# A fused attention and FFN kernel: the loop over head pairs in groups of six slots, contexts on column halves, output projection ahead in whole banks

## The chip, the cores and the metric

The kernel runs on one core of a Trainium2 chip. The metric is the device time of one execution in microseconds, a median of several runs. The five engines (TensorE, VectorE, ScalarE, GpSimd, SyncE) each take their instructions in program order and wait for one another by semaphores.

## What is computed

Two layers over x (4 x 256 tokens of 256 features, 1024 tokens in all). The change touches the first sublayer, an attention with 16 heads whose keys and values come from a context of 64 features:

```
def _L0_xattn_ref(hidden_q, kv_c, Wq, w_kc_q, w_kc_kv, W_qr, W_kr, Wo):
    q_hk = (hidden_q @ Wq.T).reshape(Bv, Sv, H, K)
    q_big = jnp.einsum('bshk,hkq->bshq', q_hk, w_kc_q)
    q_big = _apply_rope(q_big, ...)
    kv_r = _apply_rope(kv_c, ...)
    q_r = jnp.einsum('bshq,hqr->bhsr', q_big, W_qr)
    k_r = jnp.einsum('bld,hdr->bhlr', kv_r, W_kr)
    attn = jax.nn.softmax(jnp.einsum('bhsr,bhlr->bhsl', q_r, k_r), axis=-1)
    ctx_c = jnp.einsum('bhsl,bld->bhsd', attn, kv_r)
    ctx_lat = jnp.einsum('bhsd,hkd->bhsk', ctx_c, w_kc_kv)
    return ctx_lat.transpose(0, 2, 1, 3).reshape(Bv, Sv, H * K) @ Wo.T
x = x + _L0_xattn_ref(_layernorm(x), ctx_512, ...)
x = x + _L0_ffn_ref(_layernorm(x), ...)      # matmuls in emulated fp8, scales by absolute maxima
x = x + _L1_xattn_ref(ctx_512, ctx_512, mask_SxS2_bk1, mask_BxS2_bf0, _layernorm(x), ...)
x = x + _L1_ffn_ref(_layernorm(x), ...)
```

## The kernel before

Heads are taken in 8 pairs. The products of weights are folded once for each pair: `prep(f, 0)` and `prep(f, 1)` make `w1` (the two halves of Wq times w_kc_q), `prep(f, 2)` makes `wqk`, `prep(f, 3)` makes `wkvo`. All four use one PSUM bank, `pW`, in turn; ScalarE copies each out (`fold_copy`), VectorE takes the rounding rest (`w1_low`, `wqk_low`), and the next `prep` waits for that. `latent_q(m)` makes a third (r = 0, 1, 2) of the latent queries of 512 tokens in the single bank `pq`; `rope(m)` on VectorE rotates it, `join` on GpSimd adds the parts, `rope_high_xy` and `rope_high_z` on ScalarE round them, `rope_lows` on VectorE makes the rest. `latent_u(n, r)` multiplies by `wqk` into the bank `pu`; `u_copy` (ScalarE) and `u_low` (VectorE) bring it to SBUF. A unit is one head of one batch (256 x 256 scores): `scores` on TensorE, the row maximum on VectorE (L806), two exponentials on ScalarE (L549), a reciprocal on VectorE (L811), `norm_probs` on GpSimd (L392), `turn_probs` on TensorE (transposes, L1179), the copy `probT` on ScalarE (L540), and `context` on TensorE (L1191), which for the first head of a batch writes zeros into the lower half by way of zero columns kept in `kva`. VectorE copies the context of a batch to `cT` (L823). At the end `project` (L1196) multiplies `cT` by `wkvo` and sums over the 8 pairs.

The order of each engine is written out by hand: a loop `for it in range(1, PAIRS + 1)` over 12 slots of half a `latent_q` step each; in slots 1 to 8 a unit's scores are taken, three slots later it is transposed, four slots later its context comes. `latent_q` has the even slots, `latent_u` the odd slots with m % 3 below 2, `prep` slots 1, 3, 5 and 7. In the last iteration, 21 of the 64 projections (`EARLY = 3` token tiles) are spread over the slots, two calls each. After the loop TensorE projects the remaining tiles one by one, VectorE adds each to x and takes its statistics:

```
                elif i in (1, 2) and f:
                    pe.wait_ge(w1_parts, 2 * f + i)
...
            sp.wait_ge(scores_ready, NUNIT * PAIRS)
            sp.dma_start(ctx1[:], ctx_t[0:HK1, 0:TOK]).then_inc(ctx1_here, 16)
            ...
            sp.dma_start(mA[:], attn_mask.rearrange("(a p) s -> p a s", p=P)).then_inc(d_mask, 16)
```

SyncE's second piece waits for all 64 units' scores, since the tiles it fills share memory with the loop's. GpSimd, after its last `norm_probs`, waits for `d_mask`, makes the mask bias of the second attention (L430 to L436), a bias tile (L442, L443), scales `wg` (L449) and only then has the `pow` for the inverse deviation of the 1024 rows (`power(2)`, L365), for which VectorE waits in `newton(2)`.

During iterations 1 to 6 VectorE and ScalarE also find the absolute maxima of the two FFN weights and cast them to fp8 steps, in pieces (L855, L857, L568, L569).

Of the kernel before, what the change touches and what calls it, by code (L numbers as in the profile page):

```python
# [12 lines left out]
ALU = mybir.AluOpType  # L13
# [27 lines left out]
OUT_BANK = (0, 7, 2, 1, 3, 4, 5, 6)  # L41
EARLY = 3
# [5 lines left out]
GROUPS = 2 * PAIRS  # L48
HALF = DCQ // 2
# [31 lines left out]
def build(nc, x, ctx_t, ctx_n, blob, const_a, const_b, wq1_t, wk1_t, attn_mask, key_mask,  # L81
          w_fc_t, w_proj_t, small, w_router, wv_t, wo, w_gate, w_up, w_down, out):
    with ExitStack() as ctx:
# [12 lines left out]
        kva = sb("kva", [P, (2 * NT + 1) * DC])  # L96
# [258 lines left out]
        def _(pool):  # L355
# [13 lines left out]
            in_order(pool.memset(kva[:], 0.0))  # L369
# [33 lines left out]
            kv_rows = kva[:, DC:].rearrange("p (t d) -> p t d", t=NT)[:, :, 0:DC]  # L403
# [16 lines left out]
            for it in range(1, PAIRS + 1):  # L420
                for slot in range(SLOTS):
                    m = QSTEPS * it + slot // 2
                    if 2 <= slot <= NUNIT + 1:
                        norm_probs(NUNIT * (it - 1) + slot - 2)
                    if slot % 2 == 1 and m < ALLQ and m % RT:
                        join(m // RT, m % RT - 1)
# [47 lines left out]
        def _(act):  # L474
# [56 lines left out]
            for it in range(1, PAIRS + 1):  # L531
                f, g = it, it - 1
                for slot in range(SLOTS):
                    m = QSTEPS * it + slot // 2
                    if 4 <= slot <= NUNIT + 3:
                        n = NUNIT * g + slot - 4
                        act.wait_ge(probsT_ready, n + 1)
                        if n >= 2:
                            act.wait_ge(pv_ready, n - 1)
                        act.copy(probT[n % 2][:].rearrange("p a s -> p (a s)"), pT[:]).then_inc(probsT_copied, 1)  # L540
                    if 1 <= slot <= NUNIT:
                        n = NUNIT * g + slot - 1
                        act.wait_ge(max_ready, n + 1)
                        if n >= PROBS:
                            act.wait_ge(probsT_ready, n - PROBS + 1)
                        elif n == PROBS - 1:
                            act.wait_ge(kva_ready, 1)
                        for st in range(2):
# [4 lines left out]
                    if slot % 2 == 0 and m < ALLQ and m % RT == 2:  # L553
                        rope_high_xy(m // RT)
                    if slot % 2 == 0 and m < ALLQ + RT and m % RT == 0:
                        rope_high_z(m // RT - 1)
# [932 lines left out]
```

## Time and profile before

| | |
|---|---|
| median of 3 runs | 506.76 us (506.63 to 507.72) |
| profiled execution | 507.15 us, span 505.4 us |
| busy: TensorE, VectorE, ScalarE, GpSimd | 408.4, 353.0, 230.5, 201.5 us |
| loop of seven pairs | 42.9 to 279.0 us |
| last scores issued | 297.3 us |
| GpSimd's second `pow` starts | 327.0 us |

The profile shows one execution. A timeline row gives start, duration, engine, line, and what ended the idle time before it. Matmuls are pipelined: a row's duration reaches over the start of the next one, so the pitch, the distance between starts, is what an instruction costs its engine. An fp32 matmul call appears as two instructions.

### The profile page before, as it was taken

The page shows a single profiled execution, that of the slowest core. Times are in us where ns is not written, and L with a number is a line of the kernel's source. Part 1 is how long each engine was busy: PE and PEld are TensorE (multiplying, and loading weights), DVE is VectorE, ACT ScalarE, POOL GpSimd, SP SyncE. Part 2 cuts the span into 40 slices and gives each one's busy share as a digit, 9 for nine tenths or more (in the row PEclk, how much of TensorE's full clock was granted, in tenths as well). Part 3 has the DMA queues.
Part 4 walks back from the last instruction along what each step waited for, and adds up shares of the span by engine and source line. Part 5 has one row for each costly group of instructions (what it writes and reads, how often), then busy time and mean ns, then how long its engine had stood idle before and what let it go on. Part 6 is the DMA issues. An engine that isn't in the chain of part 4 may idle for free.

```text
span 505.4 us, 5862 instructions
## 1 busy us (share of the span) xinstructions
PE 408.4 (81%) x1900; PEld 299.5 (59%) x1901; DVE 353.0 (70%) x765; ACT 230.5 (46%) x562; POOL 201.5 (40%) x150
## 2 busy tenths in 40 slices
PE   2956997999897988998989999929645058969997
PEld 2735776777786877777767888613423044524465
DVE  4996869868779699697786626474699966582322
ACT  1432653756666657666566550135792123311100
POOL 2582642644545627555566449771001110040000
PEclk9976999999999999999999999965895577979999
DMA  8633020020100200000200012000000000000011
GB/s 324 211 102 148 1 84 0 1 84 3 44 40 0 85 1 1 0 2 8 108 1 0 2 50 99 1 0 1 0 0 0 1 1 0 0 1 1 0 42 42
DMA packets 8941, 18.82 MB, mean 37 GB/s; under 512 B 2128, under 2 KB 6672, under 8 KB 7760
## 3 DMA queue, kind: packets, MB, share of 16 engines
q1 hardware_dynamic: 8912, 18.46, 10.6%
q8 instruction: 15, 0.25, 0.2%
q14 instruction: 14, 0.11, 0.1%
HBM read 17.40 MB, written 1.05 MB: 37 GB/s over the span
## 4 chain that ended last, share of the span: by engine, by line
PE 54%; DVE 26%; issue 7%; ACT 7%; POOL 4%; DMA 2%; SPq 0%; POOLq 0%; DVEq 0%; ACTq 0%
PE bank L1191 10%; PE bank L1196 5%; PE bank L1380 5%; PE bank L1398 5%; PE bank L1179 4%; PE bank L1090 4%; PE bank L1092 4%; PE bank L1091 4%; PE bank L1166 3%; POOL rot_low L387 2%; DVE negmax L806 2%; DVE tail_all L1011 2%; PE bank L1296 2%; PE bank L1085 2%; DVE qr L751 2%
## 5 line engine op out<-in xcount | busy, mean ns | idle before, releaser
L392 POOL TENSOR_TENSOR prob<-prob,rinv 128x512 f32<-128x512 f32 x64 | 77.0, 1203 | 104.5 <-DVE rinv L811 104.4
L549 ACT ACTIVATE prob<-bank,negmax 128x256 f32<-128x256 f32 x128 | 59.6, 470 | 53.2 <-DVE negmax L806 53.0
L1191 PE MATMUL bank<-probT,kva 128*128 128x256 f32 x256 | 68.2, 388 | 14.1 <-ACT probT L540 13.5
L1191 PEld LDWEIGHTS bank<-probT,kva 128*128 128x128 f32 x256 | 46.4, 189 | 27.9 <-ACT probT L540 20.8
L806 DVE TENSOR_REDUCE negmax<-bank 128x2 f32<-128x512 f32 x64 | 43.9, 685 | 18.3 <-PE bank L1166 18.2
L365 POOL TENSOR_TENSOR c_y<-c_ve,minus_half 128x4 f32<-128x4 f32 (+1 forms) x10 | 12.4, 1244 | 101.7 <-DVE c_ve L686 76.3
L540 ACT COPY probT<-bank 128x512 f32<-128x512 f32 x64 | 37.7, 588 | 22.5 <-PE bank L1179 21.4
L1380 PE MATMUL bank<-tailT,blobs 128*128 128x512 f32 (+1 forms) x96 | 45.7, 633 | 1.1 <-ACT tailT L479 0.8
L1166 PE MATMUL bank<-kvT,uT 128*128 128x256 f32 x256 | 45.7, 300 | 0.3
L1090 PE MATMUL bank<-xnT,w 128*128 128x512 f32 x96 | 40.3, 420 | 1.8 <-DVE rot_low L733 1.8
L1179 PE MATMUL bank<-ca,prob 128*128 128x128 f32 x256 | 38.8, 274 | 0.5 <-POOL prob L392 0.5
L1092 PE MATMUL bank<-xnT,w 128*128 128x512 f32 x96 | 38.2, 398 | 0.0
L1166 PEld LDWEIGHTS bank<-kvT,uT 128*128 128x128 f32 x256 | 36.1, 190 | 3.3 <-issue 1.0
L1091 PE MATMUL bank<-xnT,w 128*128 128x512 f32 x96 | 38.0, 396 | 0.0
L387 POOL TENSOR_TENSOR rot_low<-rot_low,rot_up 128x1024 f32<-128x1024 f32 x15 | 37.4, 2494 | 0.3 <-DVE rot_up L736 0.3
L1179 PEld LDWEIGHTS bank<-ca,prob 128*128 128x128 f32 x256 | 31.2, 141 | 7.9 <-issue 2.3
L1380 PEld LDWEIGHTS bank<-tailT,blobs 128*128 128x128 f32 (+1 forms) x96 | 18.0, 193 | 26.6 <-issue 26.0
L385 POOL TENSOR_TENSOR rot_z<-rot_z 128x512 f32<-128x512 f32 x15 | 24.5, 1634 | 19.6 <-DVE rot_z L742 19.6
L823 DVE COPY cT<-bank 128x256 f32<-128x256 f32 x32 | 13.5, 423 | 24.2 <-PE bank L1191 23.7
L1196 PE MATMUL bank<-wkvo,cT 128*128 128x256 f32 x128 | 29.6, 379 | 0.0
L1113 PE MATMUL bank<-blobs 128*128 128x192 f32 x64 | 15.1, 365 | 15.0 <-DMA blobs<-in_blob 10.0
L1196 PEld LDWEIGHTS bank<-wkvo,cT 128*128 128x128 f32 x128 | 23.6, 190 | 2.9
(205 smaller groups left out, 851.5 us busy)
## 6 DMA issues: line engine op xcount, KB each, us to landing
blobs<-in_blob SPq DMA_DIRECT2D x8, 1024.0 KB, 5.0
xs<-in_x SPq DMA_DIRECT2D x2, 512.0 KB, 4.0
ctxT<-in_ctx_t SPq DMA_DIRECT2D x1, 1024.0 KB, 13.2
xn<-in_w_fc_t SPq DMA_DIRECT2D x1, 1024.0 KB, 4.9
ctxT<-in_w_proj_t SPq DMA_DIRECT2D x1, 1024.0 KB, 5.4
out<-qk SPq DMA_DIRECT2D x8, 128.0 KB, 1.7
cb<-in_const_b SPq DMA_DIRECT2D x1, 768.0 KB, 9.1
blobs<-in_w_gate SPq DMA_DIRECT2D x1, 704.0 KB, 4.4
```

Source lines behind the costliest of these rows:

```text
L387: pool.tensor_tensor(low, low, up, ALU.add).then_inc(joined, 1)
L392: pool.tensor_tensor(p[:], p[:], rinv[:, n % PROBS, :].unsqueeze(2).to_broadcast([P, 2, S]), ALU.mult).then_inc(normed, 1)
L549: ins = act.activation(prob[n % PROBS][:, st, :], pS[n % 2][:, st * S:(st + 1) * S], ACT.Exp, bias=negmax[:, n % 2, st:st + 1], accum_out= ...
L806: dve.tensor_reduce(negmax[:, n % 2, :], pS[n % 2][:].rearrange("p (a s) -> p a s", a=2), AX, ALU.max, negate=True).then_inc(max_ready, 1)
L1090: pe.matmul(o, a[0], b[0], start=start, stop=False)
L1091: pe.matmul(o, a[0], b[1], start=False, stop=False)
L1092: return pe.matmul(o, a[1], b[0], start=False, stop=stop)
L1166: ins = pe.matmul(pS[n % 2][:, st * S:(st + 1) * S], uT[b // 2][:, h, at:at + P], kvT[i][:, b * S:(b + 1) * S], start=(i == 0), stop=(i == 1))
L1179: ins = pe.transpose(pT[:, lt * S + st * P:lt * S + (st + 1) * P], prob[n % PROBS][:, st, lt * P:(lt + 1) * P], ident)
L1191: ins = pe.matmul(pV[b % 2][:, 0:S], kva[:, (2 * (2 * b + lt) + 1 - h) * DC:(2 * (2 * b + lt) + 1 - h) * DC + P], probT[n % 2][:, lt, :], ...
L1196: return pe.matmul(bank[OUT_BANK[t]][:, 0:D], cT[:, f, t * P:(t + 1) * P], wkvo[:, f, :], start=(f == 0), stop=(f == PAIRS - 1))
L1380: ins = pe.matmul(bk[0:m, :], w[:, k, ft * P:ft * P + m], tailT[:, k, c * CH:(c + 1) * CH], start=(k == 0), stop=(k == DK - 1))
```

## The change

The slots are numbered through, s = 12 to 110, and everything is placed by s. Six slots now make a group of four units (slots 0, 1, 3 and 4 of the six), two groups a pair. Two heads of a batch are taken as one context, placed in slots 2 and 5: four calls, each head writing its own 64 partitions of the bank, so `kva` has no zero columns and its `memset` goes. `prep` 0 to 3 move to slots 1, 5, 7 and 11, `w1_low` and `wqk_low` two slots behind the first three. `u_low` stands behind `rope` in VectorE's slot. The projection uses four whole banks, two token tiles each; 42 calls come in s = 96 to 106, 14 in s = 107 to 110, four a slot, and only the last pair's eight (`project_last`) wait for the last contexts. VectorE adds two tiles at once (`x1_tiles`). The steps on the FFN weights' maxima move to other slots. SyncE's program and GpSimd's work after the loop are as before.

```diff
-OUT_BANK = (0, 7, 2, 1, 3, 4, 5, 6)
-EARLY = 3
+OUT_BANK = (0, 7, 2, 1)
+AHEAD = 4
+STEP = SLOTS // 2
+UNIT_AT = {0: 0, 1: 1, 3: 2, 4: 3}
+TURN_AFTER = 3
+CONTEXT_AT = 17
+LAST = STEP * (GROUPS - 1) + CONTEXT_AT + 3
+LAST_PAIR = SLOTS * PAIRS
+PREP_AT = (1, 5, 7, 11)
...
+    n, k = s // STEP - 2, UNIT_AT.get(s % STEP)
+    return 4 * n + k if k is not None and 0 <= n < GROUPS else None
...
-            in_order(pool.memset(kva[:], 0.0))
...
+                n = unit_at(s - TURN_AFTER - 1)
+                if n is not None:
+                    act.wait_ge(probsT_ready, n + 1)
+                    if n >= 2:
+                        act.wait_ge(pv_ready, n // 2)
...
+                if slot - 1 in PREP_AT and f + 1 < PAIRS:
+                    fold_copy(f + 1, PREP_AT.index(slot - 1))
+                if slot == 0 and 2 <= f < PAIRS:
+                    fold_copy(f, 3)
...
+                if s % 2 == 0 and m < ALLQ:
+                    rope(m)
+                if s % 2 == 0 and m % RT == 2 and m // RT - 1 < GROUPS:
+                    u_low(m // RT - 1)
...
+                if f + 1 < PAIRS and slot - 2 in PREP_AT[:2]:
+                    w1_low(f + 1, PREP_AT.index(slot - 2))
+                if f + 1 < PAIRS and slot - 2 == PREP_AT[2]:
+                    wqk_low(f + 1)
...
+            def x1_tiles(i):
+
+                t = 2 * i
+                dve.wait_ge(attn_ready, i + 1)
+                dve.tensor_tensor(xs[:, t:t + 2, :].rearrange("p t d -> p (t d)"), bank[OUT_BANK[i]][:],
+                                  xs[:, t:t + 2, :].rearrange("p t d -> p (t d)"), ALU.add).then_inc(x1_ready, 1)
+                dve.wait_ge(x1_ready, i + 1)
+                for a in range(2):
+                    dve.bn_stats(stats[:, t + a, :], xs[:, t + a, :])
+                dve.tensor_reduce(spread[:, 0, t:t + 2], xs[:, t:t + 2, :], AX, ALU.max)
+                return dve.tensor_reduce(spread[:, 1, t:t + 2], xs[:, t:t + 2, :], AX, ALU.min)
...
+            def context(n):
+
+                b = n % B
+                pe.wait_ge(probsT_copied, 2 * n + 2)
+                if n >= 2:
+                    pe.wait_ge(cT_copied, n - 1)
                 for lt in range(2):
-                    ins = pe.matmul(pV[b % 2][:, 0:S], kva[:, (2 * (2 * b + lt) + 1 - h) * DC:(2 * (2 * b + lt) + 1 - h) * DC + P],
-                                    probT[n % 2][:, lt, :], start=(h == 0 and lt == 0), stop=(h == 1 and lt == 1))
+                    for h in range(2):
+                        ins = pe.matmul(pV[b % 2][h * DC:(h + 1) * DC, 0:S], kva[:, 2 * b + lt, :], probT[h][:, lt, :],
+                                        start=(lt == 0), stop=(lt == 1))
...
+                if s >= LAST_PAIR:
+                    for n in range(AHEAD * (s - LAST_PAIR), AHEAD * (s - LAST_PAIR + 1)):
+                        if n < 6 * (PAIRS - 1):
+                            project_ahead(n)
...
+                if last_pair_at(s) is not None:
+                    project_last(last_pair_at(s))
+                if batch_at(s) is not None:
...
+                    context(batch_at(s))
+                if unit_at(s - TURN_AFTER) is not None:
+                    turn_probs(unit_at(s - TURN_AFTER))
```

TensorE around `prep` 2 in the middle of the loop (slot 5 before: context, `prep` 2, transposes, scores). Before:

```order
L1166 MATMUL bank1<-kvT1,uT_1 128x256
L1191 MATMUL bank5<-probT_1,kva 128x256 x2
L1119 MATMUL bank7<-blobs 128x128 x3
L1179 MATMUL bank4<-ca,prob_2 128x128 x4
L1166 MATMUL bank3<-kvT0,uT_1 128x256
```

Now (slot 7: scores, `latent_u`, `prep` 2, transposes):

```order
L1196 MATMUL bank3<-kvT1,uT_1 128x256
L1121 MATMUL bank2<-qr_0_0,wqk_1_0 128x512
L1122 MATMUL bank2<-qr_0_1,wqk_1_0 128x512
L1123 MATMUL bank2<-qr_0_0,wqk_1_1 128x512
L1150 MATMUL bank7<-blobs 128x128 x3
L1208 MATMUL bank4<-ca,prob_1 128x128 x4
L1121 MATMUL bank0<-xnT0,w1_1_0 128x512
```

The fold into bank 7 moved from behind a context to a place between `latent_u` and the transposes.

VectorE around the second `w1_low` of a pair, the two steps on `w1_0_1` or `w1_1_1` from bank 7. Before (slot 4):

```order
L776 TENSOR_TENSOR uT_1<-bank2,uT_1 64x512 x2
L740 TENSOR_TENSOR rot_z<-bank0,cb 128x512
L742 TENSOR_TENSOR rot_z<-bank0,cb 64x512 x2
L702 TENSOR_TENSOR w1_0_1<-bank7,w1_0_0 128x256
L702 TENSOR_TENSOR w1_0_1<-bank7,w1_0_0 128x128
```

Now (slots 4 to 7):

```order
L763 TENSOR_TENSOR rot_z<-bank0,cb 128x512
L765 TENSOR_TENSOR rot_z<-bank0,cb 64x512 x2
L799 TENSOR_TENSOR uT_1<-bank2,uT_1 64x512 x2
L844 RECIPROCAL rinv<-rsum 128x2
L774 TENSOR_TENSOR qr_0_1<-rot_low,qr_0_0 128x1024
L861 COPY cT<-bank5 128x256
L839 TENSOR_REDUCE negmax<-bank1 128x2
L755 TENSOR_TENSOR rot_low<-bank0,cb 128x512
L756 TENSOR_TENSOR rot_low<-bank0,cb 128x512
L839 TENSOR_REDUCE negmax<-bank3 128x2
L844 RECIPROCAL rinv<-rsum 128x2
L774 TENSOR_TENSOR qr_0_1<-rot_z,qr_0_0 128x512
```

The rows end just before the two steps from bank 7, which now come one slot group later than `rope` of z, behind the whole list.

TensorE near the last scores (the last row on `kvT` in each is unit 63). Before (slots 103 and 104):

```order
L1166 MATMUL bank<-kvT,uT 128x256 x4
L1196 MATMUL bank<-wkvo,cT 128x256 x2
L1191 MATMUL bank<-probT,kva 128x256 x2
L1179 MATMUL bank<-ca,prob 128x128 x4
L1166 MATMUL bank<-kvT,uT 128x256 x4
```

Now (slots 102 to 106; of the six projections in a row two are the first `project_last`):

```order
L1196 MATMUL bank<-kvT,uT 128x256 x4
L1226 MATMUL bank<-wkvo,cT 128x256 x4
L1208 MATMUL bank<-ca,prob 128x128 x4
L1196 MATMUL bank<-kvT,uT 128x256 x4
L1226 MATMUL bank<-wkvo,cT 128x256 x6
L1208 MATMUL bank<-ca,prob 128x128 x4
L1226 MATMUL bank<-wkvo,cT 128x256 x4
L1220 MATMUL bank<-probT,kva 64x256 x4
L1196 MATMUL bank<-kvT,uT 128x256 x4
L1226 MATMUL bank<-wkvo,cT 128x256 x4
L1208 MATMUL bank<-ca,prob 128x128 x4
L1196 MATMUL bank<-kvT,uT 128x256 x4
```

Between two units' scores stood two projections, and now stand four.

## Rows read from the trace of the kernel before

**Rows 1.** The page: TensorE's busy time, and the copy of a context.
```profile
PE 408.4 (81%) x1900; PEld 299.5 (59%) x1901; DVE 353.0 (70%) x765; ACT 230.5 (46%) x562; POOL 201.5 (40%) x150
L823 DVE COPY cT<-bank 128x256 f32<-128x256 f32 x32 | 13.5, 423 | 24.2 <-PE bank L1191 23.7
```

**Rows 2.** Busy time by stretch (length, then PE, PEld, DVE, ACT, POOL, clock, DMA).
```profile
42.90:76.20 33.30, 31.61 (x169) 26.12 (x168) 23.21 (x46) 19.70 (x55) 15.87 (x12) 0.95 0.19 64
76.20:111.70 35.50, 31.24 (x170) 25.31 (x170) 28.64 (x51) 19.45 (x54) 16.73 (x13) 1.00 0.09 30
...
180.50:214.40 33.90, 30.60 (x169) 25.22 (x169) 27.72 (x52) 22.12 (x59) 18.56 (x13) 1.00 0.00 1
...
248.30:279.00 30.70, 28.24 (x152) 22.95 (x152) 24.18 (x45) 18.39 (x49) 17.81 (x13) 1.00 0.00 1
279.00:297.30 18.30, 18.19 (x108) 16.02 (x107) 9.23 (x20) 11.34 (x36) 8.11 (x7) 1.00 0.01 1
```

**Rows 3.** Timeline of TensorE in the loop (start, duration, engine, line, operands).
```profile
203.25 0.65 PE L1123 MATMUL bank<-blobs 128*64 128x256 f32 x4
203.83 0.66 PE L1179 MATMUL bank<-ca,prob 128*128 128x128 f32 x4
...
222.86 0.92 PE L1113 MATMUL bank<-blobs 128*128 128x192 f32 x4 [1.12 <-DVE w L702]
223.61 0.60 PE L1179 MATMUL bank<-ca,prob 128*128 128x128 f32 x4
223.97 0.72 PE L1166 MATMUL bank<-kvT,uT 128*128 128x256 f32 x4
224.52 0.40 PE L1090 MATMUL bank<-xnT,w 128*128 128x512 f32 x1
...
225.67 0.39 PE L1092 MATMUL bank<-xnT,w 128*128 128x512 f32 x1
...
230.77 0.83 PE L1119 MATMUL bank<-blobs 128*128 128x128 f32 x6
```

**Rows 4.** Timeline of VectorE in the same pair.
```profile
226.04 0.15 DVE L811 RECIPROCAL rinv<-rsum 128x2 f32<-128x2 f32 x1
226.22 1.39 DVE L776 TENSOR_TENSOR uT<-bank,uT 64x512 fp32r<-64x512 f32 x2
227.64 0.69 DVE L740 TENSOR_TENSOR rot_z<-bank,cb 128x512 f32<-128x512 f32 x1
...
229.77 0.62 DVE L702 TENSOR_TENSOR w<-bank,w 128x256 fp32r<-128x256 f32 x2
230.31 0.68 DVE L806 TENSOR_REDUCE negmax<-bank 128x2 f32<-128x512 f32 x1
...
230.97 1.21 DVE L751 TENSOR_TENSOR qr<-rot_low,qr 128x1024 fp32r<-128x1024 f32 x1
```

**Rows 5.** Timeline of ScalarE in the same pair.
```profile
223.44 0.47 ACT L549 ACTIVATE prob<-bank,negmax 128x256 f32<-128x256 f32 x1 [1.29 <-DVE negmax L806]
...
224.35 1.16 ACT L517 CAST uT<-bank 64x512 fp32r<-64x512 f32 x2
225.54 0.59 ACT L540 COPY probT<-bank 128x512 f32<-128x512 f32 x1
...
227.78 1.05 ACT L503 CAST qr<-rot_low 128x1024 fp32r<-128x1024 f32 x1 [0.61 <-POOL rot_low L387]
```

**Rows 6.** After the last scores: TensorE's timeline, then the chain that ended last.
```profile
297.29 1.02 PE L1196 MATMUL bank<-wkvo,cT 128*128 128x256 f32 x4
...
305.91 18.58 PE bank L1196 x86
```

**Rows 7.** Timeline of GpSimd after the last scores.
```profile
303.97 2.78 POOL L430 TENSOR_SCALAR ktmp<-mK 128x1024 f32<-128x1024 uint8 x1 [3.42 <-DMA mK<-in_key_mask]
...
319.81 4.07 POOL L449 TENSOR_SCALAR blobs<-blobs,sm 128x704 f32<-128x704 f32 x2
327.00 1.67 POOL L365 TENSOR_TENSOR c_y<-c_ve,minus_half 128x8 f32<-128x8 f32 x1 [3.13 <-DVE c_ve L686]
```

More of the change, by code:

```diff
@@ L95, in build @@
         ctxT = sb("ctxT", [P, 2, TOK])
-        kva = sb("kva", [P, (2 * NT + 1) * DC])
+        kva = sb("kva", [P, NT, DC])
         ktmp = sb("ktmp", [P, TOK])
@@ L402, in _ @@
             cx = ctxn.rearrange("p (b a) d -> p b a d", b=B)
-            kv_rows = kva[:, DC:].rearrange("p (t d) -> p t d", t=NT)[:, :, 0:DC]
+            kv_rows = kva[:]
             ka = kv_rows.rearrange("p (b a) d -> p b a d", b=B)
@@ L419, in _ @@
             join(1, 1)
[L420 to L426, printed above, removed]
+            for s in range(SLOTS, LAST + 1):
+                m = s // 2
+                if unit_at(s - 1) is not None:
+                    norm_probs(unit_at(s - 1))
+                if s % 2 == 1 and m < ALLQ and m % RT:
+                    join(m // RT, m % RT - 1)
             pool.wait_ge(d_mask, 32)
@@ new lines, in _ @@
+            for s in range(SLOTS, LAST + 1):
+                m, f, slot = s // 2, s // SLOTS, s % SLOTS
+                n = unit_at(s - TURN_AFTER - 1)
[3 more added lines that the diff above has]
+                        act.wait_ge(pv_ready, n // 2)
+                    act.copy(probT[n % 2][:].rearrange("p a s -> p (a s)"), pT[:]).then_inc(probsT_copied, 1)
+                n = unit_at(s)
+                if n is not None:
+                    act.wait_ge(max_ready, n + 1)
+                    if n >= PROBS:
+                        act.wait_ge(probsT_ready, n - PROBS + 1)
+                    elif n == PROBS - 1:
+                        act.wait_ge(kva_ready, 1)
+                    for st in range(2):
+                        ins = act.activation(prob[n % PROBS][:, st, :], pS[n % 2][:, st * S:(st + 1) * S], ACT.Exp,
+                                             bias=negmax[:, n % 2, st:st + 1],
+                                             accum_out=rsum[:, n % PROBS, st:st + 1])
+                    ins.then_inc(probs_ready, 1)
+                if s % 2 == 0 and m < ALLQ and m % RT == 2:
+                    rope_high_xy(m // RT)
+                if s % 2 == 0 and m < ALLQ + RT and m % RT == 0:
+                    rope_high_z(m // RT - 1)
+                if s % 2 == 1 and m % RT == 1 and m // RT - 1 < GROUPS:
+                    u_copy(m // RT - 1)
+                if slot - 1 in PREP_AT and f + 1 < PAIRS:
+                    fold_copy(f + 1, PREP_AT.index(slot - 1))
+                if slot == 0 and 2 <= f < PAIRS:
+                    fold_copy(f, 3)
+                if 3 <= f < 3 + W8_PIECES // 2 and slot in (5, 11):
+                    j = 2 * (f - 3) + slot // 11
+                    half, src, _, step = w8_piece(j)
+                    act.wait_ge(wscale_ready, 1)
+                    if j >= 4:
+                        act.wait_ge(w8_ready, j - 3)
+                    act.activation(step, src, ACT.Abs, scale=wsi20[:, half:half + 1])
+                    act.activation(src, src, ACT.Copy, scale=wsi[:, half:half + 1]).then_inc(wcast_ready, 1)
@@ L1275, in largest_everywhere @@
+            project_last(B - 1)
+            pe.wait_ge(x1_ready, B)
             def largest_everywhere(n, w):
```

288 lines of the change are left out of this document (117 added, 171 removed).

## The prediction, written before the changed kernel was run

> **What bounds the kernel now.** I read the page's busy times first, then a table of busy time by stretch, then the order of single instructions on each engine in one stretch of the loop, and last the end of the loop. TensorE is busy 81% of the span [rows 1]. In the table each loop pair is one stretch: seven of them run from 42.9 to 279.0 us, 236.0 in all, and an ordinary one takes 33.9, with TensorE busy 30.6 and VectorE 27.7 [rows 2]. So neither engine alone sets the pair; they wait for each other. TensorE's stream in an ordinary pair, added up from the pitches below, is about 29.2 us, so some 4.7 us a pair is waiting. After 279.0 come the last eight score units (until 297.3), the last contexts, and 18.6 us of output projection, 86 instructions back to back at 0.216 us [rows 2, 6]. Then the statistics pass through GpSimd: its `pow` starts at 327.0 and was released by VectorE, after 3.13 us of waiting. Before that GpSimd had worked without a gap from 303.97 to 323.9 on the masks of the second attention, whose transfer SyncE issues only when the last scores are done (297.3) [rows 6, 7]. From last scores to GpSimd being free is therefore 26.6 us, to the `pow` 29.7 us. That second clock, only 3.1 us behind the first, is the one to watch.
>
> **The change, part by part.** Times are against the profiled execution, 507.15 us with a span of 505.4; the median of the shown runs is 0.4 lower.
>
> *Contexts on column halves.* Before, a unit's context is four instructions of 128 columns at 0.216, 0.86 us, and a batch (two units) 1.73. After, a batch is eight instructions of 64 columns. The one 64-column group in the loop, `prep` 3 (L1123), runs four instructions, of the same size and type, in 0.58 us: its pairs run side by side, 2 x 0.216, and 0.15 is lost before the next full-width instruction starts [rows 3]. About 0.10 is lost on entry. So a batch costs 4 x 0.216 + 0.25 = 1.11, a gain of 0.6 per batch on TensorE. If halves did not overlap it would be 1.98, a loss of 0.25; I take 1.11, since the row has the same form. The rule behind the 0.25 is in the Trainium skill, TensorEngine Tiling (Array Packing), Key Properties: a change of tiling mode drains the engine, and different tiles work independently. By that page's "up to 2x" alone, without the drain, a batch would be 0.86 and the time some 4 us less than forecast; the row speaks for the drain.
>
> *The new loop order.* Six slots are one group of four score units (0 and 1 in the first two slots, 2 and 3 in the fourth and fifth). I lay the new order out with pitches from [rows 3 to 5], first from the scores of unit 2 to the scores of unit 0 of the next group. TensorE: scores 0.47 (0.55 behind transposes), two steps of `latent_u` 1.38 (six at 0.23), transposes 0.36, scores 0.55, then `latent_q`, whose last product starts 1.15 in and takes 0.39, visible after 1.6. That is 4.35. Now `rope` of step 2 (three instructions, 2.13) and behind it `u_low` (two, 1.42) on VectorE [rows 4]: 7.9. Only then may the next scores start, for they read `u`. ScalarE comes to nearly the same: reduce seen and made by 1.5, exponentials 0.9, `u_copy` 1.2, copy 0.6, exponentials 0.9, `rope_high_xy` 1.05, copy 0.6, so the context starts at 6.7 and ends at 7.8 [rows 5]. The gain of the context is covered here: `u_low`, moved behind `rope`, is late next. This stretch is 7.9.
>
> From the scores of unit 0 to those of unit 2, second half of a pair: VectorE first finishes reciprocal 0.18, low part of `qr` 1.24, copy of the context 0.42 [rows 1], then reduce 0.60, `rope` 1.22, reduce and reciprocal 0.66, low part of z 0.60, `w1_low` 0.62: 5.5 back to back. `prep` 2, which TensorE now has in the same slot (slot 7) as VectorE has `w1_low`, waits for all of it, and behind it in TensorE's queue stand the transposes of unit 3, `latent_q`, the context and the next scores. TensorE alone would have been there at 3.45. From 5.55: `prep` 2 0.87 (0.67 in flow, 0.2 more after a wait, as L1113's 0.75 against 0.51), transposes 0.44, `latent_q` 1.38, context 1.11: 9.35. First half of a pair: `prep` 0 waits for `fold_copy` 3, which ScalarE has behind the exponentials of unit 0 and the z cast (VectorE reduce at 1.8, exponentials from 2.5 to 3.4, z cast about 0.55 as half of L503's work, fold 0.4): 4.4; then 0.75 + 0.44 + 1.38 + 1.11 = 8.05.
>
> A pair is 8.05 + 7.9 + 9.35 + 7.9 = 33.2, against 33.9. The weight-cast steps (1.3 us of VectorE) fall into slots where VectorE waits for `latent_q` anyway. Pair 1 starts without older units, at a mean granted clock of 0.95, so partly at the lower of TensorE's two levels, 1.2 GHz: 14.3 + 17.25 + 0.6 for a weight maximum = 32.1 (33.3 before [rows 2]). Pair 2 has the other maximum (0.6) and the scale exchange, where TensorE waits in slot 11 for two VectorE steps behind `u_low` (1.9): 35.7 (35.5). Pairs 3 to 6: 132.9. Pair 7 has no `prep`: there the chain transposes, copy, context on ScalarE takes over, 31.3 (30.7). Sum 232.0, so the loop gains **4.0 us**. Bounds: if VectorE and ScalarE answered at once, stretches of 6.9 and 7.9 would make a pair of 29.6 and the gain 25; if GpSimd's joins come late on top, a pair is as before or 0.7 longer and the gain is 0 or -5. I take the order's own sum, since VectorE's 5.5 us are back to back in known pitches.
>
> *Projection ahead.* Before, 18.3 us lie between slot 96 and the end of the last scores [rows 2, 6]. After, TensorE has there: 40 projections (four in each of ten slots, 17.2 us at two instructions of 0.216 each), eight scores 4.1, seven transposes 2.6, three contexts 3.3, `latent_u` 2.1, one `project_last` 0.9: 30.2. The last scores come **11.9 us** later than they would. Behind them TensorE has about 12 us (16 projections, two contexts, three transposes, two `project_last`), and VectorE then two double tiles of five instructions, some 6.5 with the aggregate: 18.7 us. The 18.6 us row of projection at the end is gone, but it now lies ahead of the event that starts the mask work.
>
> *What is late next.* GpSimd's masks: 26.6 us after the last scores, as before, and that exceeds VectorE's 18.7 by 8. So the `pow` moves from 29.7 to 26.6 after the last scores: **-3.1 us**. Everything behind it is unchanged. TensorE rests longer ahead of the next stage, which may move its clock's steps; I allow 1 us either way for it.
>
> *At one answer:* the dropped `memset` of `kva` stood at the start, where GpSimd waits for the first statistics; the double tiles save instructions off the chain.
>
> Sum: -4.0 + 11.9 - 3.1 = +4.8. 507.15 + 4.8 = 511.95, and by the median **511.6 us**.
>
> **Rivals.**
> 1. *Even distances pay more.* If `prep` 2 and `prep` 0 find their inputs ready, TensorE's own stream sets the first stretch: 1.1 and 2.4 less, 3.6 a pair, about 22 in six pairs: 490. Half of it: 500. For it: TensorE's stream is 26.8 a pair after the change. Against: the DVE order puts `w1_low` last in slot 7.
> 2. *The loop doesn't gain.* GpSimd's join of z stands ahead of the z cast, and so of `prep` 0 and `w1_low`; if it and the reduces answer later than laid out, by 0.7 to 1.3 a pair, pairs are 33.9 to 34.5: 516 to 520.
> 3. *Halves one after the other.* 1.98 a batch: 0.87 in each first stretch, 0.65 in each second, 21 in the loop and 2.6 in the end: 535. Against: L1123.
> 4. *The masks don't decide.* Were GpSimd free by VectorE's time, the `pow` would come at 18.7: 504. Against: the mask work stands ahead of the `pow` in GpSimd's queue, and its trigger is unchanged.
> The turning point for faster or slower is the loop: it must gain 8.8 us (1.3 a pair) to break even.
>
> **How the numbers follow.** Forecast, with pairs from 32.6 to 33.8: 0.58, its own range 508 to 516. Rival 1 in full 0.07, half 0.15; rival 2 0.12; rival 3 0.04; rival 4 0.04. The range 501 to 518 leaves out rival 1 in full and the low end of its half, rival 3 and the upper end of rival 2: 0.2. A measurement of this kernel tells about 0.2%, 1 us, from no change. Faster: 0.26 from rivals 1 and 4, less what ends within 1 us: 0.23. Same: 0.08, between the forecast's low end and rival 1's half. Slower: 0.69.
>
> **What would show it.** Pair length near 33.2, with waits of TensorE for `w` by VectorE in slot 7 of every pair (about 2 us) and none before `prep` 1; eight instructions of a context in about 1.1; the last scores near 305 and the `pow` 26.6 later, released by GpSimd's own queue with no wait for `c_ve`; TensorE idle in between. Wrong: pairs under 32, or a `pow` that still waits for VectorE.

## The result and the profile after

The changed kernel takes 512.36 us (median of 4, 511.52 to 513.53) where the kernel before, beside it on the same chip, takes 506.69 (505.42 to 507.72). The ratio is 1.0115, 95% interval 1.009 to 1.014: slower by 1.2%. The profiled execution took 513.53 us with a span of 511.7 (before 507.15 and 505.4). Ratios here leave out executions that lie over 1.5% above the fastest of their kernel; that matters for one experiment only, the old order with column halves, where the spread is itself a finding.

The page, against [rows 1]: the engines' busy times, the context, and VectorE's copy of it.

```profile
PE 389.6 (76%) x1901; PEld 265.2 (52%) x1901; DVE 354.4 (69%) x753; ACT 224.8 (44%) x562; POOL 202.5 (40%) x149
...
L1220 PE MATMUL bank<-probT,kva 128*64 128x256 f32 x256 | 34.7, 392 | 15.7 <-ACT probT L561 15.7
...
L861 DVE COPY cT<-bank 128x256 f32<-128x256 f32 x32 | 13.5, 421 | 17.2 <-PE bank L1220 16.8
```

TensorE lost 19 us of busy time, and the kernel got slower: it was not TensorE's load that set the end. The same table by stretch as [rows 2] (length, then PE, PEld, DVE, ACT, POOL, clock, DMA), with pairs 1, 2, 3, an ordinary one, pair 7 and the stretch to the last scores:

```profile
43.10:74.90 31.80, 26.85 (x155) 20.62 (x153) 24.66 (x46) 17.88 (x52) 14.90 (x10) 0.96 0.16 50
74.90:110.40 35.50, 27.77 (x168) 20.96 (x168) 28.06 (x52) 18.89 (x54) 19.53 (x13) 1.00 0.04 16
110.40:144.90 34.50, 30.14 (x175) 22.12 (x173) 26.26 (x51) 21.44 (x58) 16.81 (x12) 0.95 0.13 42
...
178.20:211.50 33.30, 28.17 (x169) 20.77 (x169) 28.04 (x53) 21.26 (x58) 18.19 (x12) 1.00 0.05 22
...
244.70:276.30 31.60, 25.43 (x151) 18.56 (x151) 24.94 (x45) 17.30 (x49) 18.18 (x12) 1.00 0.10 41
276.30:307.10 30.80, 30.80 (x178) 25.47 (x179) 12.13 (x26) 12.40 (x38) 9.80 (x8) 1.00 0.01 1
```

An ordinary pair takes 33.3 where it took 33.9, with TensorE busy 28.2 instead of 30.6. Pair 3 takes 34.5 at a mean clock of 0.95. The last stretch has grown from 18.3 to 30.8 us, with TensorE busy in all of it. Then GpSimd's timeline behind the last scores, against [rows 7], and the two rows of VectorE beside its last ones:

```profile
313.56 2.78 POOL L453 TENSOR_SCALAR ktmp<-mK 128x1024 f32<-128x1024 uint8 x1 [2.69 <-DMA mK<-in_key_mask]
...
329.36 4.06 POOL L472 TENSOR_SCALAR blobs<-blobs,sm 128x704 f32<-128x704 f32 x2
333.38 1.67 POOL L390 TENSOR_TENSOR c_y<-c_ve,minus_half 128x8 f32<-128x8 f32 x1
```

```profile
325.74 0.61 DVE L709 TENSOR_SCALAR c_ve<-mv 128x8 f32<-128x8 f32 x1
...
335.16 0.17 DVE L699 TENSOR_TENSOR c_t<-c_y 128x8 f32<-128x8 f32 x1 [7.17 <-POOL c_y L390]
```

(`c_ve` is VectorE's last result of the statistics, the input of the `pow`; `c_y` is what the `pow` hands back.) Before, the `pow` had waited 3.13 us for `c_ve`; now it follows GpSimd's own queue without a wait, `c_ve` has been there since 326.35, and VectorE waits 7.17 for the `pow`. The 6.3 us between the two spans add up in four pieces. The loop ends at 276.3 instead of 279.0: -2.7. From there to the last scores 30.8 against 18.3: +12.5. From the last scores (307.1) to the `pow` (333.4) 26.3 against 29.7: -3.4. From the `pow` to the end of the span 178.3 against 178.4: -0.1.

### The profile page after: what moved, and what is told of

The parts are those of the page before. It is cut to its first block, busy times and chain, and to the rows that moved or that the text cites. A ratio compares the mean times of both kernels' runs of the same rounds, so it can differ in the third digit from the quotient of the medians.

```text
span 511.7 us, 5850 instructions
## 1 busy us (share of the span) xinstructions
PE 389.6 (76%) x1901; PEld 265.2 (52%) x1901; DVE 354.4 (69%) x753; ACT 224.8 (44%) x562; POOL 202.5 (40%) x149
## 4 chain that ended last, share of the span: by engine, by line
PE 46%; DVE 32%; POOL 8%; issue 7%; ACT 3%; DMA 2%; SPq 1%; POOLq 0%; DVEq 0%; ACTq 0%
PE bank L1419 5%; PE bank L1437 5%; PE bank L1196 4%; PE bank L1121 4%; PE bank L1123 4%; PE bank L1122 4%; PE bank L1220 4%; PE bank L1226 4%; DVE rot_z L765 3%; DVE uT L799 3%; PE bank L1208 3%; DVE qr L774 3%; POOL prob L416 2%; DVE tail_all L1042 2%; PE bank L1335 2%
## 5 line engine op out<-in xcount | busy, mean ns | idle before, releaser
L416 POOL TENSOR_TENSOR prob<-prob,rinv 128x512 f32<-128x512 f32 x64 | 84.8, 1326 | 116.0 <-DVE rinv L844 115.6
L1196 PE MATMUL bank<-kvT,uT 128*128 128x256 f32 x256 | 47.4, 308 | 3.6 <-DVE uT L799 3.6
L1220 PE MATMUL bank<-probT,kva 128*64 128x256 f32 x256 | 34.7, 392 | 15.7 <-ACT probT L561 15.7
L411 POOL TENSOR_TENSOR rot_low<-rot_low,rot_up 128x1024 f32<-128x1024 f32 x15 | 36.0, 2398 | 16.5 <-DVE rot_up L759 16.4
L1208 PE MATMUL bank<-ca,prob 128*128 128x128 f32 x256 | 38.9, 274 | 2.8 <-ACT probT L561 2.8
L1220 PEld LDWEIGHTS bank<-probT,kva 128*64 128x64 f32 x256 | 15.6, 136 | 31.1 <-ACT probT L561 19.2
L570 ACT ACTIVATION_READ_ACCUMULATOR prob<-bank,negmax 128x1 f32 x128 | 25.9, 202 | 0.0
```

Source lines behind the costliest of these rows:

```text
L416: pool.tensor_tensor(p[:], p[:], rinv[:, n % PROBS, :].unsqueeze(2).to_broadcast([P, 2, S]), ALU.mult).then_inc(normed, 1)
L570: ins = act.activation(prob[n % PROBS][:, st, :], pS[n % 2][:, st * S:(st + 1) * S], ACT.Exp, bias=negmax[:, n % 2, st:st + 1], accum_out= ...
L1196: ins = pe.matmul(pS[n % 2][:, st * S:(st + 1) * S], uT[b // 2][:, h, at:at + P], kvT[i][:, b * S:(b + 1) * S], start=(i == 0), stop=(i == 1))
L1208: ins = pe.transpose(pT[:, lt * S + st * P:lt * S + (st + 1) * P], prob[n % PROBS][:, st, lt * P:(lt + 1) * P], ident)
L1220: ins = pe.matmul(pV[b % 2][h * DC:(h + 1) * DC, 0:S], kva[:, 2 * b + lt, :], probT[h][:, lt, :], start=(lt == 0), stop=(lt == 1))
```

## The experiments

Three questions were put to the chip: does the mask work of GpSimd really turn the projection ahead into a loss, what in the loop costs what, and why does pair 3 take 1.2 us more than its neighbours.

### The end of the first sublayer

**The power ahead of work that nobody waits for.** GpSimd's bias tile and the scaling of `wg` (about 5.8 us between the masks and the `pow`) go behind it:

```diff
-            pool.wait_ge(d_small, 16)
-            pool.wait_ge(rot_ready, ALLQ)
-            for k in range(DK):
-                ...
-            pool.wait_ge(d_ffn1, 64)
-            scale_rows(wg)
             power(2, c_ve[:], minus_half[:], c_y[:])
             ...
+            pool.wait_ge(d_small, 16)
+            ...
+            scale_rows(wg)
             scale_rows(wu)
```

> The changed kernel, with GpSimd's order after the loop altered: the second pow and the eight normalised tiles come right behind the mask bias, and the bias tile and the scaling of wg and wu behind them. Nothing before that changes. Theory (GpSimd's work after the last scores decides when the pow starts): the 5.8 us of bias tile and scaling leave the chain; the pow starts at about 327.6 instead of 333.4 us of the profile, and the time falls by about 5.7 to 506.7. VectorE's own statistics, ready at 326.35, are then the next bound, 1.3 us below. Rival (the place where the pow stands doesn't matter, the loss is in the loop): the time stays at 512.4.

Measured: 507.28 us, ratio to the kernel before 0.9998 (0.9977 to 1.0018). GpSimd's timeline:

```profile
327.68 1.29 POOL L459 TENSOR_TENSOR mbias<-mbias,ktmp 128x512 f32<-128x512 f32 x1
328.93 1.66 POOL L390 TENSOR_TENSOR c_y<-c_ve,minus_half 128x8 f32<-128x8 f32 x1
```

The `pow` follows the last mask, 20.8 us behind the last scores (308.1 in this execution) instead of 26.3: the `pow` comes 5.5 us sooner, with the loop untouched. Of the time 5.1 us is back by the medians of the two kernels (512.36 and 507.28), and 5.9 by their ratios to the kernel before that ran beside each. GpSimd's queue was the path.

**The same edit in the kernel before**, where VectorE's statistics come last:

> The kernel before, with the same edit of GpSimd's order as the first run of this set (pow and normalised tiles ahead of the bias tile and the scaling). There the pow already waits 3.1 us for VectorE, so the theory expects the same time as before, within 0.5 us. If the edit gains some 5 us here too, the change of order helps for another reason than the one named.

Measured: 507.2 us, ratio 0.9991 (0.9969 to 1.0013), no difference. One edit is worth 5 us in one kernel and nothing in the other; what it is worth depends on which of the two chains ends last, GpSimd's masks or VectorE's statistics.

**The masks' transfers first.** The trigger of the masks: behind the last scores SyncE issues its transfers one after the other, and GpSimd waits for the fourth and fifth.

```diff
             sp.wait_ge(scores_ready, NUNIT * PAIRS)
+            sp.dma_start(mA[:], ...).then_inc(d_mask, 16)
+            sp.dma_start(mK[:].rearrange("p b s -> p (b s)"), ...).then_inc(d_mask, 16)
             sp.dma_start(ctx1[:], ctx_t[0:HK1, 0:TOK]).then_inc(ctx1_here, 16)
             ...
```

> The changed kernel, with SyncE's two mask transfers issued ahead of the three for ctx1 and the two small weights. Theory (the chain is last scores, mask transfer, GpSimd's masks, pow): the mask of keys lands about 1.8 us earlier, the time of three issues, and the pow and the end follow by 1.8: 510.5. Rival (GpSimd isn't started by the transfer, or the pow waits for something else): no change, 512.4.

Measured: 511.15 us, ratio 1.0069 (1.0043 to 1.0095). The first mask instruction now waits 0.32 us for its data in place of 2.69, since GpSimd is busy with the last `norm_probs` until then, and the `pow` comes 24.0 us behind the last scores: 2.3 earlier, a little more than expected.

```profile
314.71 2.78 POOL L453 TENSOR_SCALAR ktmp<-mK 128x1024 f32<-128x1024 uint8 x1 [0.32 <-DMA mK<-in_key_mask]
```

**The projection later.** Two projections a slot in s = 96 to 105 instead of four, the rest behind the last scores:

```diff
-AHEAD = 4
+ENDS = [2 * i for i in range(11)] + [28, 35, 42, 49, 56]
...
-                    for n in range(AHEAD * (s - LAST_PAIR), AHEAD * (s - LAST_PAIR + 1)):
-                        if n < 6 * (PAIRS - 1):
-                            project_ahead(n)
...
+                    i = s - LAST_PAIR
+                    for n in range(ENDS[i], ENDS[i + 1]):
+                        project_ahead(n)
```

> The changed kernel, with the 56 projections ahead dealt out anew: two instead of four in each slot 96 to 105, the rest (eight, then seven a slot) in slots 106 to 110, so TensorE's work is the same in sum but 20 projections (8.6 us) less stand before the last scores. Theory: the last scores are issued at 298.4 instead of 307.1 us, GpSimd is free at about 324.8, and now VectorE's statistics, unmoved at 326.3, release the pow: 333.4 becomes about 326.5, the time 505.5. Rival (the projections before the last scores are not what delays the pow): 512.

Measured: 507.29 us, ratio 0.9992 (0.9972 to 1.0013). The last scores end at 299.1, and both chains end together: GpSimd's queue is empty at 326.6, and `c_ve` is there at 326.7.

```profile
322.58 4.06 POOL L472 TENSOR_SCALAR blobs<-blobs,sm 128x704 f32<-128x704 f32 x2
326.75 1.67 POOL L390 TENSOR_TENSOR c_y<-c_ve,minus_half 128x8 f32<-128x8 f32 x1
```

The same 56 projections, dealt out otherwise, take the 5 us back. The profiled execution (505.37) meets the 505.5 that was expected, the median is 1.8 above it: the ten executions go from 504.50 to 508.70, and what sets them apart was not followed up. TensorE's work up to `c_ve` is the same wherever the projections stand; only the event that starts the masks moves (`c_ve` is there at 326.67 here and at 326.35 in the changed kernel).

### The loop

**`prep` 2 one slot later.** `prep` 2 in slot 8 of TensorE, so that it no longer stands in front of the transposes and `latent_q` while it waits for `w1_low`:

```diff
+PE_PREP_AT = (1, 5, 8, 11)
...
-                if slot in PREP_AT and f + 1 < PAIRS and (f, slot) != (2, 11):
-                    prep(f + 1, PREP_AT.index(slot))
+                if slot in PE_PREP_AT and f + 1 < PAIRS and (f, slot) != (2, 11):
+                    prep(f + 1, PE_PREP_AT.index(slot))
```

> The changed kernel, with prep 2 on TensorE one slot later (slot 8, behind latent_q, ahead of the context) and nothing moved on the other engines. It takes away the wait of 2.1 us for w1_low in the second half of six pairs. Theory (several chains stand close behind each other): the transposes of unit 3 then wait for ScalarE's copy of unit 2, which comes at about 5.1 us after the group's first scores, so that stretch falls only from 9.1 to about 8.7 and the whole time by 2.4 to 510. Rival (the wait named in the profile is all that stands there): the stretch falls to 7.0 and the time by 12 to 500.

Measured: 512.21 us, ratio 1.0104 (1.0052 to 1.0156), against 1.0115 of the changed kernel: no difference that these runs can tell, and too wide an interval to rule the expected 2.4 us in or out. The second half's first stretch went from 9.09 to 8.76 us, and TensorE's wait there moved to the transposes, which want `probT` (1.39 us). The wait for `w1_low` is real but shallow; another stands right behind it. In the profiled execution an ordinary pair took 33.0, but pair 2 took 36.2 instead of 35.5, with a mean granted clock of 0.62 from 108 to 112 us, where the changed kernel had 0.78. So part of the 2 us that six pairs gave went to the clock in that execution; whether in the others too isn't shown.

**`u_low` ahead of `rope`**, as the kernel before had it:

```diff
-                if s % 2 == 0 and m < ALLQ:
-                    rope(m)
                 if s % 2 == 0 and m % RT == 2 and m // RT - 1 < GROUPS:
                     u_low(m // RT - 1)
+                if s % 2 == 0 and m < ALLQ:
+                    rope(m)
```

> The changed kernel, with u_low ahead of rope in VectorE's slot, as the kernel before had it. Theory (u_low ends the stretch from unit 2's scores to the next group by 0.1 to 0.2 us over ScalarE's chain, and VectorE's backlog of recip, low part and copy sets the next stretch): stretch 2 falls from 8.02 to about 7.85, and because VectorE is free 0.4 earlier, stretch 1 by 0.35; about 1.0 a pair, 6 to 7 in all: 506. Rival (ScalarE's chain binds alone): 512; rival (rope's result comes later and costs more than u_low gains): above 512.4.

Measured: 508.38 us, ratio 1.0021 (0.9985 to 1.0056), where the changed kernel had 1.0115: 4.0 us less by the medians, where 6 to 7 were expected, with executions from 504.95 to 512.18. The pair:

```profile
176.20:208.40 32.20, 28.07 (x171) 20.79 (x169) 28.21 (x52) 21.28 (x59) 18.16 (x13) 1.00 0.07 28
```

33.3 became 32.2, as expected in sum. The shares were not as expected: the stretch from unit 2 to the next unit 0 gave 0.42 (8.02 to 7.60), each of the two others only 0.08 to 0.17. Two instructions on VectorE in the wrong place (2 x 0.71 us) were worth as much as the column halves, as the next one shows.

**Full width in the new order.** The contexts as before, with zero columns, everything else as in the changed kernel:

```diff
...
-                for lt in range(2):
-                    for h in range(2):
-                        ins = pe.matmul(pV[b % 2][h * DC:(h + 1) * DC, 0:S], kva[:, 2 * b + lt, :], probT[h][:, lt, :],
-                                        start=(lt == 0), stop=(lt == 1))
+                for h in range(2):
+                    for lt in range(2):
+                        at = (2 * (2 * b + lt) + 1 - h) * DC
+                        ins = pe.matmul(pV[b % 2][:, 0:S], kva[:, at:at + P], probT[h][:, lt, :],
+                                        start=(h == 0 and lt == 0), stop=(h == 1 and lt == 1))
```

> The changed kernel with only the column halves undone: a batch's context is four calls of 128 columns with the zero columns in kva, in the same place. Theory: a batch costs TensorE 1.73 instead of 1.11; the first stretch of a group grows by 0.62, the second by about 0.45 (0.17 of it was covered by u_low), 15 in the loop and 2 before the last scores: about 529. Rival (the context is covered in the new order, its halves bring nothing): within 2 us of 512.4.

Measured: 525.54 us, ratio 1.036 (1.0307 to 1.0413), 3.5 under the 529 that was expected. Here are a context at full width and the start of the next scores in this kernel, and under it the same in the changed one:

```profile
201.07 1.99 PE L1222 MATMUL bank<-probT,kva 128*128 128x256 f32 x8 [0.97 <-ACT probT L562]
202.71 0.82 PE L1197 MATMUL bank<-kvT,uT 128*128 128x256 f32 x4
```

```profile
202.34 1.08 PE L1220 MATMUL bank<-probT,kva 128*64 128x256 f32 x8
203.36 0.74 PE L1196 MATMUL bank<-kvT,uT 128*128 128x256 f32 x4
```

From start to start 1.64 against 1.02 us. An ordinary pair takes 34.5 instead of 33.3: of the 4 x 0.62 that four batches save on TensorE, half reaches the pair. Of the 13 us in the total, 11.4 are there at slot 96; 3.4 of these are pair 2, which took 38.9 and ends at half clock, so not all of the 13 is the contexts' own time.

**Column halves in the old order.** The kernel before with only its contexts changed, both heads of a batch at once in slots 5, 7, 9 and 11:

```diff
...
-                    if 4 <= slot <= NUNIT + 3:
-                        if it == 1 and slot == 4:
+                    if slot >= 5 and slot % 2 == 1:
+                        if it == 1 and slot == 5:
                             pe.wait_ge(kva_ready, 1)
-                        context(g, slot - 4)
+                        context(g, (slot - 5) // 2)
```

> The kernel before with its own loop order and its own projection, and only the contexts changed: both heads of a batch at once on column halves, in slots 5, 7, 9 and 11. My theory: with the changed kernel full width instead of halves cost about 13 us over 32 batches, 0.41 of the 0.62 that a batch takes less on TensorE; in the old order too TensorE and VectorE wait for each other, so a part of the saving is covered. I expect 0.2 to 0.4 a batch, pairs of 32.3 to 33.1 where they were 33.9, and a time near 498 (494 to 501): the column halves pay as well without the new order, and the new order by itself is then a loss. Rival A: halves pay only in the new order, since in the old one VectorE or GpSimd closes the pair: 505 to 508. Rival B: all of TensorE's saving is on the path: 2.5 a pair, 487 to 489.

Measured: 504.86 us, but from 498.74 to 508.55 in 12 executions; ratio 0.9919 (0.9885 to 0.9954). The profiled execution (499.22) meets the 498 that was expected; the median is some 7 us off. In that execution pairs 3 and 4 took 32.8 each, inside the range expected, but pairs 5 and 6 took 34.4, and the trace shows why: the clock. It is the question of the changed kernel's pair 3, too.

### The clock inside the loop

TensorE in the changed kernel, at the end of pair 2, where it waits for the diagonal of the weight maxima:

```profile
104.73 0.61 PE L1208 MATMUL bank<-ca,prob 128*128 128x128 f32 x4
108.98 0.38 PE L1293 MATMUL bank<-wdiag,ca 128*128 128x2 f32 x2 [3.64 <-DVE wdiag L876]
109.30 1.12 PE L1220 MATMUL bank<-probT,kva 128*64 128x256 f32 x8
110.35 1.23 PE L1196 MATMUL bank<-kvT,uT 128*128 128x256 f32 x4
111.37 0.63 PE L1121 MATMUL bank<-xnT,w 128*128 128x512 f32 x1
111.80 0.63 PE L1122 MATMUL bank<-xnT,w 128*128 128x512 f32 x1
```

The pitch of a 512-column product is 0.43 us here, where it is 0.23 elsewhere: 1.2 GHz in place of 2.4. Before, the same wait was 0.45 us long, and the granted clock stayed at 1.0 from 48 us to the end of the loop. That agrees with what the Trainium skill says in TensorE: Matmul & The Clock Gate, Part 1: the throttled state is the default, and activity releases it.

In the old order with column halves the fall comes behind three shorter waits (0.22, 0.76 and 1.40 us):

```profile
189.42 0.74 PE L1165 MATMUL bank<-kvT,uT 128*128 128x256 f32 x4 [0.76 <-DVE uT L775]
191.55 1.56 PE L1190 MATMUL bank<-probT,kva 128*64 128x256 f32 x8 [1.40 <-ACT probT L539]
193.04 1.65 PE L1118 MATMUL bank<-blobs 128*128 128x128 f32 x6
```

**TensorE kept busy in its waits.** Three kernels test it: products whose result nobody reads, into the unused half of the next context's bank, placed ahead of the waits.

```diff
+            def fill(n, calls):
+                pe.wait_ge(cT_copied, max(n - 1, 0))
+                for _ in range(4 * calls):
+                    pe.matmul(pV[n % 2][:, S:2 * S], kvT[0][:, 0:P], kvT[0][:, 0:S], start=True, stop=True)
...
                 if f == 2 and slot == 11:
+                    fill(batch_at(s), 7)
                     pe.wait_ge(wdiag_ready, 1)
```

First the old order with column halves, filled in three waits of each pair:

> The old loop order with column halves (as in e9), and TensorE kept busy in three waits of each pair: 8 products that nobody reads ahead of prep 0 (wait 1.10), 12 ahead of the context in slot 5 (wait 1.40), 8 ahead of the one in slot 11 (wait 1.21). The runs of e9 lie between 498.7 and 508.6, the long ones at a lower mean granted clock (0.895 against 0.907), and its profiled execution had a stretch at 0.5 from 191.5 to 195 right behind two waits, which cost 1.6. My theory: the spread is the clock's, which falls in some waits of the loop; with them filled nearly all executions lie at 498.5 to 501, median near 500, and the column halves alone are then worth 7 us. Rival: the spread has another source and stays: median 503 to 506. Or the filling itself costs 0.3 a pair: 502 to 503 without spread.

Measured: 499.59 us (497.64 to 502.39, 6 executions), ratio 0.9846 (0.9811 to 0.9881). The same stretch of time in the same pair, in the second fence with the filling (PE, PEld, DVE, ACT, POOL, clock, DMA):

```profile
187.00:191.00 4.00, 2.18 (x12) 1.30 (x10) 3.90 (x8) 3.35 (x10) 3.49 (x2) 1.00 0.01 4
191.00:195.00 4.00, 3.45 (x17) 2.54 (x18) 3.23 (x7) 1.52 (x6) 2.11 (x2) 0.63 0.00 0
```

```profile
187.00:191.00 4.00, 3.02 (x19) 2.23 (x18) 3.89 (x7) 3.34 (x12) 4.00 (x3) 1.00 0.00 0
191.00:195.00 4.00, 4.00 (x33) 3.30 (x33) 3.94 (x8) 2.72 (x8) 1.60 (x2) 1.00 0.01 4
```

The clock stays at 1.0 through the loop, every ordinary pair takes 32.8, and the long executions are gone. 28 products a pair that nobody reads made the kernel 5.3 us faster by the medians (504.86 and 499.59). Not all of the spread was the loop's clock: the six executions still lie in two groups, three near 498 and three from 501.0 to 502.4. The column halves alone, with the clock held, are worth 8.3 us by the medians (499.59 against 507.86 beside it). The profiled execution, one of the longer of the six, shows 5.8 of them in its span.

Then the changed kernel, filled:

> The changed kernel with TensorE kept busy where it waits: products of 128x256 whose result nobody reads, into the unused half of the next context's bank, 28 of them (about 3.0 us) in slot 11 of pair 2, where it waited 3.64 us for the diagonal of the maxima, and 12 (about 1.3 us) ahead of prep 2 in slot 7 of pairs 2 to 6, where it waited 1.63. The profiled execution of the changed kernel had a granted clock of 1.0 in the loop but for about 110.4 to 113.6 us, right behind the long wait, where it was 0.5, and there pair 3 took 34.5 in place of 33.3. My theory: the wait makes the clock fall; with the filling it stays at 1.0 from 48 us to the end of the loop, pair 3 takes 33.3, and the time is 1.2 less, near 511. Rival: the filling lies on the path or disturbs the wait's end, 512.5 to 515, or the clock falls there all the same, 512.4.

Measured: 513.05 us (511.74 to 513.51, 4 executions), ratio 1.0104 (1.0074 to 1.0134). The clock:

```profile
104.00:108.00 4.00, 4.00 (x33) 3.79 (x32) 3.30 (x6) 2.77 (x7) 1.04 (x1) 1.00 0.01 2
108.00:112.00 4.00, 3.71 (x25) 2.64 (x23) 3.55 (x9) 0.00 (x0) 3.07 (x2) 1.00 0.01 2
112.00:116.00 4.00, 3.98 (x26) 2.86 (x25) 3.28 (x7) 3.21 (x11) 1.23 (x2) 1.00 0.49 147
```

It no longer falls, pair 3 takes 33.4 instead of 34.5, and slot 96 begins at 275.0 instead of 276.3. So the mechanism is as supposed, but the 1.2 us can't be seen in the total, whose median is 0.7 higher than the changed kernel's and whose ratio is 0.001 lower: four executions of each kernel lie 2 us apart, and of this one 178.9 us of the span lie behind the `pow` instead of 178.3.

### All of it together

The three single edits of the changed kernel that paid (the power first, the projection later, `u_low` ahead of `rope`) at once, first as they are:

> Three single edits of the changed kernel made at once: GpSimd's power ahead of the bias tile and the scaling of wg and wu; 22 projections (two a slot) in s = 96 to 105 and seven each in s = 107 to 110; u_low ahead of rope on VectorE. My theory: the loop ends 5.3 us earlier, as with u_low ahead alone (slot 96 at 271.0 against 276.3); last scores then near 299.1 - 5.3 = 293.8; the masks are done 19.9 to 20.5 us behind them, at about 314; the power therefore waits for VectorE's statistics, which end at 326.7 - 5.3 = 321.4; from there 178.3 to the end of the span, 499.7, and a time near 501.5, 5 us under the kernel before. Rival: the gains don't add, since TensorE's stream behind the last scores (34 projections) or a clock step in its rest holds the statistics at 324 or later: 504 to 506.

Measured: 501.01 us (499.40 to 506.15, 12 executions), ratio 0.9904 (0.9873 to 0.9936). The expected 501.5 is met. The gain of the loop adds to the one behind it; the power first and the projection later do not add to each other, since both shorten the same wait for the `pow` (5.1, 5.1 and 4.0 us by the medians one by one, 11.4 together). But the profiled execution (504.45) had two stretches at half clock, at 97 to 101 us and at 111 to 115. With the filling:

> The three edits of e8 together, with the filling of e10. The runs of e8 lie between 499.4 and 506.2, six of twelve above 501.5, and its profiled execution had two stretches at a granted clock of 0.5, at 97 to 101 and at 111 to 114, each behind a wait of TensorE in pair 2. My theory: filled, the executions lie at 499 to 500.5, median near 499.8, 7 us under the kernel before. Rival: the waits' clock is not the source: median 501 and the same spread.

Measured: 500.72 us (499.81 to 501.45, 6 executions), ratio 0.9864 (0.984 to 0.9888): none of the six is as long as the upper half of the twelve, the middle is as good as unmoved, 0.9 above what was expected. It is 1.4% faster than the kernel before and, by the two ratios, 2.5% faster than the changed one. GpSimd's `pow` waits for VectorE again, and for long:

```profile
311.81 1.26 POOL L459 TENSOR_TENSOR mbias<-mbias,ktmp 128x512 f32<-128x512 f32 x1
320.01 1.67 POOL L390 TENSOR_TENSOR c_y<-c_ve,minus_half 128x8 f32<-128x8 f32 x1 [6.93 <-DVE c_ve L709]
```

So the mended new order and the old order with column halves end some 1 us apart (500.7 and 499.6), within the spread of either.

## Why the prediction was right, point by point

The time was forecast at 511.6 and came at 512.4; slower was given 0.69. It was right for the reason it gave, the trade behind slot 96, and most steps can be read off the trace. Its sums hold, to 0.1 us of rounding (the terms of the first half's first stretch add up to 8.08, not 8.05).

- **The context.** Forecast 1.11 a batch, measured 1.02 from start to start, and some 0.09 on entry. The row of `prep` 3 [rows 3] had the right form and the right price. Rival 3 (halves one after the other) is out, by the row and by the experiment at full width.
- **The pair.** Forecast stretches 8.05, 7.9, 9.35, 7.9; measured 8.14, 8.02, 9.09, 8.04, in sum 33.3 against 33.2, so rival 2 (33.9 or more) is out. The waits were those named:

```profile
199.65 0.94 PE L1150 MATMUL bank<-blobs 128*128 128x128 f32 x6 [1.66 <-DVE w L725]
...
209.95 1.08 PE L1220 MATMUL bank<-probT,kva 128*64 128x256 f32 x8 [1.04 <-ACT probT L561]
211.40 0.74 PE L1196 MATMUL bank<-kvT,uT 128*128 128x256 f32 x4 [0.37 <-DVE uT L799]
...
215.88 0.89 PE L1144 MATMUL bank<-blobs 128*128 128x192 f32 x4 [0.73 <-ACT wkvo L515]
```

`prep` 2 waits for `w1_low` by 1.66 (forecast: about 2), the scores of the next group for `u_low`, and `prep` 0 for ScalarE's `fold_copy` 3. The text said that `u_low` is late next in its stretch; putting it back gave 1.1 a pair. What it had too large is the weight of the wait for `w1_low`: rival 1 took 2.4 a pair for it (9.35 down to TensorE's own 6.95), and moving `prep` 2 freed 0.33.
- **The loop, mis-sized.** Forecast 232.0, measured 233.2 (43.1 to 276.3), so the loop itself gained 2.9 and, begun 0.2 later, ended 2.7 earlier, not 4.0. What is missing is pair 3 (34.5 against 33.2); the other pairs missed by 0.1 to 0.3 each, up and down, and cancel. The step that failed is that of pair 2: it had TensorE waiting in slot 11 and priced the wait alone. That price, 1.9, came out (the stretch with the wait took 9.97, the same stretch of an ordinary pair 8.04). The fall of the clock behind it was not in the sum, and the next stretch, the first of pair 3, took 9.37 instead of 8.14. The trace of before could have warned: from 328 to 336 us TensorE was busy for 2.1 of the 8 us, and the granted clock was 0.5 from 336 to 352, also while TensorE was busy again. The filled kernel's pair 3 (33.4) settles that.
- **Slot 96 to the last scores.** Forecast 30.2, measured 30.8, TensorE busy throughout; which of its parts hold the 0.6 was not looked into.
- **Last scores to the `pow`.** Forecast 26.6, GpSimd's own time, with VectorE ready after 18.7; measured 26.3 and 19.3 (326.35 - 307.1). Rival 4 is out, and the two experiments on GpSimd's order, one in each kernel, show which chain decides in each. The 1 us allowed for the clock of the next stage wasn't needed: 178.3 against 178.4.
- **The turning point.** The text put it at a loop gain of 8.8 us. With `u_low` ahead of `rope` slot 96 came 8.0 earlier (271.0 against 279.0), and the ratio was 1.0021 (0.9985 to 1.0056), not to be told from 1.

Set side by side, the ordinary pairs part the change of the loop into its pieces, in us: kernel before 33.9; column halves alone 32.8; the new order alone 34.5; both, as changed, 33.3; both with `u_low` in its old place 32.2. Column halves are worth 1.1 to 1.2 a pair in either order. The new order costs 0.5 to 0.6 as it was written, and gains 0.6 once those two instructions are put back. What stays open is what that 0.6 would be at the end: the two kernels that could tell (500.7 and 499.6) differ in their last part too.

## What to carry over

Work that is moved ahead of an event fills an engine and delays whatever that event starts: before moving it, follow each chain that starts at the event, here a transfer and 20 us of mask work on an engine that is otherwise off the path. When two chains meet at one instruction, move only as much as lies between them; the same projections dealt out later cost nothing. And when a saving on TensorE turns into waiting, look at its granted clock stretch by stretch before judging the edit: part of the gain may be hidden by a clock that the new waits let fall, and filling them with idle products, a dozen lines, can bring it back.

## What the runs showed of the hardware

- The clock fell to half behind a single wait of 3.64 us (changed kernel), and behind three waits of 0.22, 0.76 and 1.40 us in a row (old order with halves). It didn't fall behind one of 3.06 us in the kernel with `u_low` ahead, nor behind the same three in pairs 3 and 4 of the other, so it is not the wait's length alone that decides. The Trainium skill tells of such a case in another kernel, in TensorE: Matmul & The Clock Gate, A second HAM failure mode: psum-queue depth-cycling: frequent short idles between groups of products can make the clock go to and fro. These traces agree in kind. What it cost here: 1.1 us for pair 3, 1.6 for each of pairs 5 and 6, and most of a spread of 10 us between executions of the old order with halves, which fell to 4.8 with the waits filled; the kernel before, beside it, has 4.
- Idle products of 128x256 in a wait did not delay what followed where they ended before the wait did: the diagonal's product started 4.36 us behind the transposition of the maxima with them and without.
- Two 64-column products on different halves of the array ran side by side: eight instructions of 256 columns took 1.02 us from the start of the first to the start of what follows, against 1.64 for the eight at full width.
